# A top-k cross attention: score weights by one 32-line transfer and two copying engines, TensorE's filler without a gap, and context columns requested ahead of inputs 6 and 7

## The reference

```python
scores = einsum('bnd,d->bn', x, score_w[0]) + score_b[0]
_, topk_idx = top_k(scores, 10)
q = (x[topk_idx] @ Wq.T + bq)          # 10 queries, 16 heads of 32
k = (ctx @ Wk.T + bk);  v = (ctx @ Wv.T + bv)
o = softmax(q k^T / sqrt(32)) v
out = x;  out[topk_idx] = o @ out_w.T + out_b
```

## Time and profile before

| | |
|---|---|
| median of three runs | 142.82 us (142.78 to 142.98) |
| profiled execution | 142.91 us, span 141.1 us |
| TensorE busy | 134.8 us, 96% of the span |
| VectorE busy | 80.7 us, 57% |
| ScalarE busy | 25.7 us, 18% |
| GpSimd busy | 6.4 us, 5% |
| bytes moved by transfers | 37.52 MB, 266 GB/s over the span |
| granted TensorE clock, mean | 0.994 |

### The profile page before, as it was taken

One profiled execution on the slowest core, in us unless ns is written; L12 is line 12 of the kernel. 1 busy time (PEld: TensorE's weight loads), 2 busy tenths in 40 slices (PEclk: granted clock), 3 DMA queues, 4 the chain that ended last, 5 costly groups with the idle time before them and its releaser, 6 DMA issues.

```text
span 141.1 us, 3075 instructions
## 1 busy us (share of the span) xinstructions
PE 134.8 (96%) x1314; PEld 127.8 (91%) x1314; DVE 80.7 (57%) x212; ACT 25.7 (18%) x56; POOL 6.4 (5%) x31
## 2 busy tenths in 40 slices
PE   6998998999999999999999999999999999999990
PEld 4567996999999989999999999999999999998970
DVE  2987546898960576288880674088128605754350
ACT  4311410030412250003140041005001400411110
POOL 7500000003000000000000000000000000000002
PEclk9999999999999999999999999999999999999997
DMA  4999999999996199999989985995880281000001
GB/s 146 410 405 422 406 417 399 438 422 431 428 335 286 39 359 395 288 398 424 433 294 310 313 334 157 314 321 230 261 298 17 46 359 45 0 0 5 0 5 49
DMA packets 6959, 37.52 MB, mean 266 GB/s; under 512 B 961, under 2 KB 961, under 8 KB 4642
## 3 DMA queue, kind: packets, MB, share of 16 engines
q1 hardware_dynamic: 6528, 37.00, 69.2%
q0 software_dynamic: 128, 0.33, 0.7%
q10 hardware_dynamic: 290, 0.01, 0.1%
HBM read 33.50 MB, written 3.83 MB: 265 GB/s over the span
## 4 chain that ended last, share of the span: by engine, by line
PE 77%; DMA 12%; SPq 4%; issue 2%; DVE 1%; POOLq 1%; POOL 0%; DVEq 0%
PE mix_ps L794 37%; PE logits_ps L775 23%; DMA ctx_c<-ctx_cols_dram 12%; PE logits_ps L761 10%; SPq L202 3%; PE logits_ps L725 2%; PE logits_ps L691 1%; PE mix_ps L725 1%; SPq L195 1%; POOLq L60 1%; DVE o_T L548 1%; PE misc_ps L809 1%; DVE heads L545 1%; PE misc_ps L743 0%; PE logits_ps L809 0%
## 5 line engine op out<-in xcount | busy, mean ns | idle before, releaser
L794 PE MATMUL mix_ps<-probs,ctx_r 125*128 125x160 f32 x384 | 54.2, 300 | 0.0
L794 PEld LDWEIGHTS mix_ps<-probs,ctx_r 125*128 125x128 f32 x384 | 52.6, 190 | 0.6 <-issue 0.5
L775 PE MATMUL logits_ps<-qk,ctx_c 128*125 128x160 f32 x240 | 33.4, 299 | 0.0
L775 PEld LDWEIGHTS logits_ps<-qk,ctx_c 128*125 128x125 f32 x240 | 32.9, 188 | 0.0
L496 DVE TENSOR_REDUCE col_max<-logits_ps 125x160 f32<-125x960 f32 x8 | 9.2, 1153 | 25.1 <-PE logits_ps L775 21.3
L761 PE MATMUL logits_ps<-qk,ctx_c 128*125 128x160 f32 x144 | 20.8, 302 | 0.7 <-DMA ctx_c<-ctx_cols_dram 0.7
L761 PEld LDWEIGHTS logits_ps<-qk,ctx_c 128*125 128x125 f32 x144 | 19.7, 188 | 1.7 <-issue 1.0
L349 ACT ACTIVATE mix<-mix_ps 128x320 f32<-128x320 f32 x16 | 7.0, 440 | 64.9 <-PE mix_ps L794 64.9
L534 DVE TENSOR_REDUCE prob_sum<-probs 125x160 f32<-125x960 f32 x8 | 14.6, 1839 | 4.0 <-ACT probs L345 4.0
L345 ACT ACTIVATE probs<-probs 125x480 f32<-125x480 f32 x16 | 9.3, 603 | 27.8 <-DVE probs L528 27.8
L397 DVE CUSTOM_DVE_ANT_0 product<-x_sb,score_w_sb 112x513 f32<-112x513 f32 x16 | 10.4, 692 | 4.4 <-DMA x_sb<-x_lines_dram 4.3
(11 more groups left out here) (121 smaller groups left out, 88.7 us busy)
## 6 DMA issues: line engine op xcount, KB each, us to landing
ctx_r<-ctx_rows_dram SPq DMA_DIRECT2D x8, 1536.0 KB, 7.5
ctx_c<-ctx_cols_dram SPq DMA_DIRECT2D x6, 1500.0 KB, 10.2
x_sb<-x_lines_dram SPq DMA_DIRECT2D x8, 520.0 KB, 10.0
out_dram<-x_sb SPq DMA_DIRECT2D x8, 448.0 KB, 11.2
ctx_c<-ctx_cols_dram SPq DMA_DIRECT2D x2, 750.0 KB, 14.7
ctx_c<-ctx_cols_dram SPq DMA_DIRECT2D x4, 375.0 KB, 16.3
wq_sb<-wq_dram SPq DMA_DIRECT2D x1, 1024.0 KB, 7.8
wk_sb<-wk_dram SPq DMA_DIRECT2D x1, 1024.0 KB, 10.6
```

Of the source, the lines that this page charges most:

```text
L775: last = nc.tensor.matmul(logits_ps[n][0:S_P, t // BANK_T, (t % BANK_T) * HQ:(t % BANK_T + 1) * HQ], ctx_c[n][:, f, t, :], qk[:, b, f, :], ...
L794: last = nc.tensor.matmul(mix_ps[half][:, f * HQ:(f + 1) * HQ], ctx_r[n][0:S_P, t, c:c + P], probs[n][:, t, :], start=(t == 0), stop=(t == ...
```

## The change

The change has four parts.

1. **Score weights.** SyncE's first transfer now fetches the line of 512 weights into 32 partitions at once (64 KB written). VectorE copies these 32 partitions on to partitions 32 to 63 and 64 to 95, ScalarE copies 16 of them to partitions 96 to 111 (`high_w_done`), and VectorE waits for both before `score(0)`. TensorE has no part in it any more. `ones` and PSUM are not used, and `score_line` is gone.
2. **Input 0** is issued by ScalarE, as its first transfer, in place of the 2 KB line.
3. **Filler.** The matmul of 256 columns, the wait and the four spreading matmuls are gone. `keep_warm` issues two matmuls of 512 columns one behind the other.
4. **Order.** SyncE issues part f = 3 of batch 0 ahead of input 6 and part f = 0 of batch 1 ahead of input 7; both stood behind them. VectorE takes `find_max(0, 0)` ahead of `score(7)`.

```diff
--- before.py
+++ after.py
@@ -41,7 +41,7 @@
 CB = HQ // QUAD
 QUADS = P // QUAD
 QK_UNITS = 2 * QK_STEPS
-WARM_WEIGHTS, WARM_SCORES, WARM_RANKS, WARM_PARTS = (256,), (512,), (256, 128), (128,)
+WARM_SCORES, WARM_RANKS, WARM_PARTS = (512, 512), (256, 128), (128,)
 X_ROW = D + 8
 LEAST = 1.401298464324817e-45
 FIRST = GROUPS[0][1]
@@ -77,7 +77,6 @@
         out_b_sb = sb("out_b_sb", [P, DT])
         y_T = sb("y_T", [P, DT, BQ])
         score_w_sb = sb("score_w_sb", [X_P, D + 1])
-        score_line = sb("score_line", [1, D])
         ctx_c = [sb(f"ctx_c{n}", [P, DT, S_T, S_P]) for n in range(2)]
         ctx_r = [sb(f"ctx_r{n}", [P, S_T, D]) for n in range(2)]
         ident = sb("ident", [P, P])
@@ -139,7 +138,6 @@
         fold_ps = mix_ps + misc_ps
         pair_ps = [[logits_ps[1][:, 0, :], logits_ps[1][:, 1, :]], mix_ps]
         key_ps = [logits_ps[1][:, 0, :], misc_ps[0][:, :]]
-        score_w_ps = mix_ps + misc_ps
         y_T_ps = [logits_ps[0][:, 0, 0:2 * BQ], mix_ps[1][:, 0:BQ], misc_ps[1][:, 0:BQ]]
         y_rows_ps = [logits_ps[0][0:BQ, 1, 0:D // 2], mix_ps[0][0:BQ, 0:P], logits_ps[1][0:BQ, 0, 0:P]]
         scores_ps = misc_ps[1][0:GB, 0:N]
@@ -159,7 +157,7 @@
         consts_cleared, numbers_done, vec_consts = sem("consts_cleared"), sem("numbers_done"), sem("vec_consts")
         ident_done, edge_done, own_done, ties_done, hot_cleared = sem("ident_done"), sem("edge_done"), sem("own_done"), sem("ties_done"), sem("hot_cleared")
         regroup_done, mask_done = sem("regroup_done"), sem("mask_done")
-        score_w_ps_done, score_w_done = sem("score_w_ps_done"), sem("score_w_done")
+        score_w_done, high_w_done = sem("score_w_done"), sem("high_w_done")
         scored, scores_T, topk_step = sem("scored"), sem("scores_T"), sem("topk_step")
         diag_done, spread_done, ranked = sem("diag_done"), sem("spread_done"), sem("ranked")
         idx_diag_done, idx_moved, idx_ready = sem("idx_diag_done"), sem("idx_moved"), sem("idx_ready")
@@ -204,7 +202,8 @@
             def copy_x(b):
                 sp.dma_start(out_pairs[:, b, :, :], x_sb[0:X_P, b, :, 0:D]).then_inc(x_copied, 16)
 
-            load_x(0, 3)
+            sp.dma_start(score_w_sb[0:QUAD, 0:D], score_row.broadcast_to([QUAD, D])).then_inc(score_w_in, 16)
+            load_x(1, 3)
             sp.dma_start(wq_sb[:, :, :], wq).then_inc(wq_in, 16)
             load_x(3, 4)
             sp.dma_start(wk_sb[:, :, :], wk).then_inc(wk_in, 16)
@@ -212,10 +211,10 @@
             load_cols_part(0, 0)
             load_x(5, 6)
             load_cols_part(0, 1)
+            load_cols_part(0, 2)
             load_x(6, 7)
-            load_cols_part(0, 2)
+            load_cols_part(1, 0)
             load_x(7, 8)
-            load_cols_part(1, 0)
             load_cols_part(1, 1)
             load_cols_part(1, 2)
             load_rows(0, 0)
@@ -293,7 +292,7 @@
 
         @block.scalar
         def _(act):
-            act.dma_start(score_line[:, :], score_row).then_inc(score_w_in, 16)
+            act.dma_start(x_sb[:, 0, :, :], x_lines[0, :, :, :]).then_inc(x_in[0], 16)
             act.dma_start(bias_sb[:, :, :], in_bias).then_inc(bias_in, 16)
 
             def spread_diag():
@@ -352,6 +351,8 @@
 
             act.wait_ge(vec_consts, 1)
             nc.scalar.activation(act_woken[:, :], ones[0:16, 0:1], ACT.Identity)
+            act.wait_ge(score_w_in, 16)
+            nc.scalar.activation(score_w_sb[3 * QUAD:X_P, 0:D], score_w_sb[0:X_P - 3 * QUAD, 0:D], ACT.Copy).then_inc(high_w_done, 1)
             spread_diag()
             copy_parts()
             copy_queries(0)
@@ -384,10 +385,11 @@
         @block.vector
         def _(dve):
             def copy_score_w():
-                for r in range(DT):
-                    dve.wait_ge(score_w_ps_done, r + 1)
-                    nc.vector.tensor_copy(score_w_sb[:, r * P:(r + 1) * P], score_w_ps[r][0:X_P, 0:P]).then_inc(score_w_done, 1)
-                dve.wait_ge(score_w_done, DT)
+                dve.wait_ge(score_w_in, 16)
+                for k in range(1, 3):
+                    nc.vector.tensor_copy(score_w_sb[k * QUAD:(k + 1) * QUAD, 0:D], score_w_sb[0:QUAD, 0:D]).then_inc(score_w_done, 1)
+                dve.wait_ge(score_w_done, 2)
+                dve.wait_ge(high_w_done, 1)
 
             def score(b):
                 dve.wait_ge(x_in[b], 16)
@@ -586,8 +588,8 @@
             score(5)
             copy_key_dot(0)
             score(6)
+            find_max(0, 0)
             score(7)
-            find_max(0, 0)
             find_shift(0)
             subtract_max(0, 0)
             choose_eight()
@@ -618,12 +620,6 @@
                     nc.tensor.matmul(logits_ps[1][:, 1, 0:n], ones[:, :], ones[:, 0:1].broadcast_to([P, n]),
                                      start=True, stop=True)
 
-            def spread_score_w():
-                pe.wait_ge(score_w_in, 16)
-                for r in range(DT):
-                    nc.tensor.matmul(score_w_ps[r][0:X_P, 0:P], ones[0:1, 0:X_P], score_line[:, r * P:(r + 1) * P],
-                                     start=True, stop=True).then_inc(score_w_ps_done, 1)
-
             def spread_scores(b):
                 for j in range(2):
                     pe.wait_ge(diag_done, 2 * b + j + 1)
@@ -831,8 +827,6 @@
                     last.then_inc(y_ps, 1)
 
             pe.wait_ge(vec_consts, 1)
-            keep_warm(WARM_WEIGHTS)
-            spread_score_w()
             keep_warm(WARM_SCORES)
             spread_scores(0)
             spread_scores(1)
```

## The result

Over 22 executions of each, the changed kernel takes 1.0035 times as long as the kernel before (95% interval 1.0025 to 1.0046), 0.50 us on 142.83. Six of its 22 executions (146.7 to 147.1 us) and one of the 22 before (146.0 us) are of a slower kind that every ratio here leaves out, and of the two profiles of that kind, of the swapped queues and of the decoupled kernel, I use nothing behind 10 us. The profiled execution took 143.32 us; the median of all 22 is 143.56, that of the other 16 is 143.46. The forecast was 142.7, with a range to 143.05.

The account below looks back on a forecast made before the run. Bound: batch 0's rows landing at 31.3; plus 0.1 (64 KB) and 0.05 (wait), `weigh(0)` starts at 31.45 against 31.57, 0.1 us sooner. 142.91 less 0.1 is 142.8, median 0.09 lower: 142.7; own range 142.55 to 142.9, 8-in-10 range 142.35 to 143.05.

Parts of the forecast that it names:

- The bound: Start of `weigh(0)`: the landing of batch 0's rows at 31.3 limits the new order's gain to 0.12 to 0.27 us.
- Filler as such: TensorE's front: four filler records end at about 5.3 us, not much after the first diagonal could come, so cost nothing.
- The copies: Score weights within SBUF before `score(0)`: VectorE's two take 0.44 to 1.36 us, ScalarE's about 0.6, done at 3.9.
- Rival B: Wait at L667 for `idx_diag`: late front puts VectorE's chain behind the row numbers; 0.3 us later, 143.1; chance 0.13.
- Input 0 and the copies: Front: weights land by 3.2, VectorE's copies end at 4.1, input 0 lands at 4.8, `score(0)` starts 0.1 us later.
- the term d: Front's shift, moving the start of batch 0's logits from 17.04: 0.1 us later, bounds -0.4 to +0.9.
- The score weights' transfer: SyncE's first load: 64 KB less 2 KB delays every later landing by 0.1 us, bounds 0 and 0.15.
- rival A: Loads' ramp: fills by up to 0.27 us, rows land at 31.1, stalls stay gone; 0.45 us gained, 142.4; chance 0.22.
- what hides what: Front before `weigh(0)`: shifts between -0.4 and +0.4 us change nothing, hidden by the stall at f = 1 and the 27.6 landing.
- The wait of the transposes for `score(7)`: TensorE after eight matmuls of batch 1: arrives at 26.1, `score(7)` ends at 26.3; 0.2 us, hidden before 27.6.
- TensorE's readiness: Before `weigh(0)`: f = 2-3 lands at 27.6, twelve matmuls take 3.26 us, ready at 30.9, 0.67 us earlier than 31.57.

Follow-up runs that it names:

- the swapped queues: Changed kernel with its two first issues swapped: input 0 first in SyncE's queue, the 64 KB first in ScalarE's; ratio to before 1.0048.
- the decoupled kernel: Changed kernel with score transposes after 14 instead of 8 matmuls, row numbers after 8 instead of 5; ratio to before 1.0029.
- the better version: Kernel before with part 4's order, rows of batch 0 in two transfers, row numbers after 7 matmuls instead of 5; ratio 0.9954, median 142.19 us.

## Why the prediction was wrong

**What held.** The bound was read rightly: the rows' landing, in no list of waits, stops the gain of the new order (order alone 1.0002; with the rows split and the row numbers asked for later 0.9954). f = 3 and f = 0 no longer stall TensorE. Filler as such cost nothing. The copies were rightly sized: VectorE 0.87 us for both, ScalarE's took 0.63, ending at 4.71. Rival B, given 0.13, is what came in its size and its cause, a late front with the maximum ahead of `score(7)`. Its place was another: the row numbers were there at 33.31, 0.1 us before TensorE came to L663, so TensorE did not wait for them but for `score(7)` at the transposes (L633), and for the rows.

**First step that failed: "Input 0 and the copies", the term d.** I took +0.1 us, with bounds -0.4 and +0.9; d was +1.01. Of it 0.66 us is `score(0)`'s late start. I put the weights' landing at 3.2 at the latest, by the bytes between it and input 0, as if they shared one queue; it was 4.0 on two, and 2.8 on one. Input 0 landed at 5.2 where I took 4.8. The other 0.35 us is TensorE's level. The Trainium skill (TensorE: Matmul & The Clock Gate, section Why this matters for your kernels) asks for no long idle gap between bursts of matmuls, or the clock returns to the lower level. The trace agrees in kind: TensorE was idle from 4.7 to 6.6 and busy for 0.41, 0.40 and 0.34 us of the next three half microseconds, and the granted clock was 0.50 at 8.0. The gap was shorter than the one that the page warns of. I had looked at whether the filler ends too late, never at whether it ends too early; my sum had it end at 5.3, and it ended at 4.7.

**Second step: "The score weights' transfer".** I took 0.1 us on the rows' landing (bounds 0 and 0.15); it was about 0.55. The profiles group: without the 64 KB the rows landed at 31.3, 30.9, 31.1 and 31.2 (before, order alone, rows split, input 0 from ScalarE), with them in one queue at 31.5 and 31.6, with them beside input 0 on another queue at 31.9, 31.8, 32.1, 31.9, 31.5 and 31.7. The means are 31.1, 31.55 and 31.8. So it costs 0.4 us in one queue and 0.7 in two, of which the bytes are 0.16, and these are single profiles that differ by up to 0.6 among themselves. The ramp is where it is lost; I had looked there only for a gain, in rival A.

**Third: what hides what.** I let d up to 0.4 be hidden and gave the chance of more only 0.13. Then I put the two waits into different rivals. They ended together, at 31.9 and 31.95, and no removal of one alone showed a gain clear of noise. The wait of the transposes for `score(7)`, 0.2 us in my working, I had put inside the wait for batch 1's last part at 27.6. That part landed at 28.2 to 28.3, and TensorE, which resumed its logits at 27.50, needed it only four matmuls later, at 28.6: nothing was left to hide the wait. With both waits gone the late logits took no more than the order's gain: begun at 18.09, 1.05 us late, they led to `weigh(0)` at 31.59, the time of before, where 30.9 was TensorE's readiness by my working.

**What stays open.** How the 0.50 us divides can't be told, as either wait alone may give nearly all of it. Why the order alone gained nothing in twelve executions, when its profile has `weigh(0)` 0.63 us sooner, is open too: the rows' wait in that profile is 0.2 us, and the better version is 0.7 us ahead of it by the ratios. Why 112 partitions load more slowly was not tried. Nor do I know how much of d is by chance of the execution: picking took 1.44 us in this profile, 1.94 in another, at lateness that differed little.

## What to carry to other kernels

When the wait that you remove ends only tenths ahead of another, price both, and look for landings that nobody waits for yet; here the new order gained nothing by itself, and 0.7 us with a transfer split so that work could start on its first half and the row numbers asked for later. A change at the very start is paid for by every load behind it and by TensorE's clock: keep the first, urgent load at the head of the queue that carries the backlog, and carry filler up to the moment at which real matmuls come, not to a fixed count. Two waits that end together can be told apart only with a kernel that has neither.

## What the runs showed of the hardware

- A 520 KB load on ScalarE's queue, issued 0.1 us behind SyncE's second load (1.36 against 1.26), took 7.9 us, and that one 5.6. The queues did not share evenly.
- Loads of 112 partitions moved 338 GB/s, of 128 partitions 412, both at a share of 1.02 to 1.03 of busy transfer engines.
- The granted clock's column says 1.00 in several profiles where TensorE's rows say otherwise: picking took 1.94 us with the column at 1.00 (the 64 KB alone), and 1.08 us in the kernel with more filler. Only where the clock fell within the profile, as at 8.0 us above, does the column show it. In the first 10 us the durations are the better witness.
- VectorE's two copies of 512 float32 elements within SBUF took 0.87 us together, 0.4 each: less than the 0.68 each that the score's 1.2 ns an element would give, the prediction's upper bound.
